# A graph network kernel: twelve node tiles moved to the next gather stage, and a sum moved into a PSUM bank

## The reference

```python
x = _layernorm(x + layer(x, src, dst, ...), axis=-1)
```

## Time and profile before

| what | value |
|---|---|
| median of 3 runs | 2564.44 us (2561.69 to 2572.5) |
| the profiled execution's own time | 2570.28 us |
| its span, first to last instruction | 2568.5 us |
| DVE busy | 1866.1 us (73%) |
| POOL busy | 1429.4 us (56%) |
| PE busy | 1363.8 us (53%) |
| ACT busy | 795.8 us (31%) |
| mean granted PE clock | 0.761 |

### The profile page before, as it was taken

One profiled execution on the slowest core, in us unless ns is written; L12 is line 12 of the kernel. 1 busy time (PEld: TensorE's weight loads), 2 busy tenths in 40 slices (PEclk: granted clock), 3 DMA queues, 4 the chain that ended last, 5 costly groups with the idle time before them and its releaser, 6 DMA issues. The chain is left out here.

```text
span 2568.5 us, 25903 instructions
## 1 busy us (share of the span) xinstructions
PE 1363.8 (53%) x5738; PEld 822.6 (32%) x5738; DVE 1866.1 (73%) x3900; ACT 795.8 (31%) x1636; POOL 1429.4 (56%) x1382
## 2 busy tenths in 40 slices
PE   2443333444766657776467577635888552424241
PEld 1332333332444433332233454411333221212120
DVE  3887777776999957776788699977888675555552
ACT  1232222223666635453122355531232110101010
POOL 6777777745777457773000577720000277777776
PEclk9556666566999979998688799976888665566665
DMA  5433333331333222221011344420000010111110
GB/s 174 121 111 109 110 109 94 107 103 50 93 85 96 75 68 75 75 74 43 22 39 39 88 129 130 126 71 20 28 27 27 29 23 23 24 23 23 23 22 13
DMA packets 120397, 174.74 MB, mean 68 GB/s; under 512 B 36128, under 2 KB 42382, under 8 KB 120340
## 3 DMA queue, kind: packets, MB, share of 16 engines
q1 hardware_dynamic: 74836, 129.98, 15.1%
q0 software_dynamic: 43904, 43.81, 8.7%
q10 hardware_dynamic: 1600, 0.33, 0.1%
HBM read 88.48 MB, written 86.74 MB: 68 GB/s over the span
## 5 line engine op out<-in xcount | busy, mean ns | idle before, releaser
L461 POOL DMA_INDIRECT GA<-table,look_i x588 | 613.1, 1043 | 495.4 <-PEq L1569 213.6
L467 PE MATMUL P<-ident,GA 128*128 128x128 f32 x500 | 104.2, 345 | 404.4 <-DMA GB<-in_x,dst_i 197.3
L491 PE MATMUL P<-center,work 128*128 128x128 f32 x800 | 150.8, 348 | 213.1 <-DVE work L1793 175.7
L266 POOL DMA_INDIRECT GA<-in_x,src_i x196 | 210.2, 1072 | 82.9 <-issue 70.1
L1733 POOL DMA_INDIRECT out_x<-work,seg_i x196 | 205.9, 1051 | 59.8 <-issue 59.8
L1725 POOL DMA_INDIRECT GA<-table,look_i x196 | 201.0, 1026 | 59.8 <-issue 59.4
L266 POOL DMA_INDIRECT GB<-in_x,dst_i x196 | 196.4, 1002 | 59.7 <-issue 59.7
L515 ACT ACTIVATE work<-P 128x512 f32<-128x512 f32 x100 | 59.5, 595 | 512.2 <-PE P L491 512.2
L491 PEld LDWEIGHTS P<-center,work 128*128 128x128 f32 x800 | 133.4, 252 | 244.2 <-issue 115.3
L467 PEld LDWEIGHTS P<-ident,GA 128*128 128x128 f32 x500 | 71.8, 175 | 429.5 <-issue 208.0
L1737 POOL MEMSET GA<- 128x512 f32 x1 | 0.5, 525 | 339.4 <-POOLq L166 339.4
(11 more groups left out here) (349 smaller groups left out, 3498.1 us busy)
## 6 DMA issues: line engine op xcount, KB each, us to landing
table<-work SPq DMA_DIRECT2D x175, 256.0 KB, 2.7
XN<-in_x SPq DMA_DIRECT2D x98, 256.0 KB, 2.8
out_x<-work SPq DMA_DIRECT2D x73, 256.0 KB, 2.1
GA<-table,look_i POOLq DMA_INDIRECT x784, 2.4
XN<-in_src_pad SPq DMA_DIRECT2D x13, 512.0 KB
cols<-in_dst_pad SPq DMA_DIRECT2D x50, 128.5 KB, 4.6
table<-XN SPq DMA_DIRECT2D x1, 6400.0 KB
out_x<-GB SPq DMA_DIRECT2D x25, 256.0 KB, 3.0
```

The lines of the kernel that those rows point to most:

```text
L266: pool.indirect_dma_start(buf[:, s % 2, j * D:(j + 1) * D], None, a["x"], bass.IndirectOffsetOnAxis(ap=look[:, s * 8 + j:s * 8 + j + 1], a ...
L461: pool.indirect_dma_start(GA[:, par, j * D:(j + 1) * D], None, table_k, bass.IndirectOffsetOnAxis(ap=look[:, s * 8 + j:s * 8 + j + 1], axis=0)
L467: ins = pe.transpose(dst[:, q * 128:(q + 1) * 128], src[:, q * 128:(q + 1) * 128], ident[:, :])
L491: ins = pe.matmul(norm_bank(par, far)[:, q * 128:(q + 1) * 128], W[par][4][:, q * 128:(q + 1) * 128], center[:, :], start=True, stop=True)
```

## The change

Node tiles 3, 7, ..., 47 leave the first gather stage, which keeps tiles 1, 5, ..., 49 (13 of them, one for every second edge tile), always in the buffers of parity 0. They are done in the second gather stage, which then has 37 node tiles: its odd slots, empty before, work on every second odd tile (`lent`). In the message stage DVE no longer adds `XD` to the scanned messages; PE centres both, with twice the number of matmuls, and accumulates them in one bank (`norm_pe_sum`). It waits for the second scan in place of the sum. PE's part of that stage is written out in place of the loop. `merge` also takes streams with nothing in them.

```diff
-def paced(eng, S, nodes, owns, unrolled=False):
+def paced(eng, S, nodes, owns, unrolled=False, lent=False):
...
-            if n >= 0 and stage is not None:
+            if n >= 0 and stage is not None and not (lent and n % 4 == 1):
                 at_n, turn = (n, 0) if i is None else (4 * i + n, 2 * i)
+                turn = turn + (n // 2 + 1)
+                if lent and n % 4 == 3:
+                    turn = (0 if i is None else i) + (n // 4 + 1)
                 if not isinstance(at_n, int) or at_n < 2 * NS:
-                    going.append(stage(of(S, n % 2), at_n, n % 2, turn + (n // 2 + 1)))
+                    going.append(stage(of(S, n % 2), at_n, n % 2, turn))
...
+        def norm_pe_sum(pe, T, s, par, k):
+
+            yield 0
+            pe.wait_ge(T("scan1"), k)
+            for q in range(4):
+                part = norm_bank(par, False)[:, q * 128:(q + 1) * 128]
+                pe.matmul(part, W[par][7][:, q * 128:(q + 1) * 128], center[:, :], start=True, stop=False)
+                ins = pe.matmul(part, XD[:, bass.ds(s * HW + q * 128, 128)], center[:, :], start=False, stop=True)
+            ins.then_inc(T("centred"), 1)
...
-                return lambda T, n, par, k: stage(T, n, par, k) if is_node(n, base) and not (even and par) else None
+                return lambda T, n, par, k: stage(T, n, par, k) if is_node(n, base) else None
...
-        NX, NV = ([g[:, par, :] for par in range(2)] for g in (XN, GB))
+        NX, NV = XN[:, 0, :], GB[:, 0, :]
...
+        def beside_even(stage):
+
+            return lambda T, s, par, k: stage(T, s, par, k) if par == 0 else iter(())
...
-                pipelined(dve, S0, gate, sums, together(partial(norm_dve, dve), node_first),
-                          together(partial(back_dve, dve, bank=3), node_second))
+                pipelined(dve, S0, gate, sums, together(partial(norm_dve, dve), beside_even(node_first)),
+                          together(partial(back_dve, dve, bank=3), beside_even(node_second)))
...
                     pe.wait_ge(T("node_x"), 16 * k)
-                    older, turn = tile_before(par, k)
                     if not (isinstance(s, int) and s == 0):
-                        pe.wait_ge(S0(f"node_sq1{older}"), turn)
-                    transpose4(pe, NA, NX[par]).then_inc(T("node_xt"), 1)
+                        pe.wait_ge(T("node_sq1"), k - 1)
+                    transpose4(pe, NA, NX).then_inc(T("node_xt"), 1)
...
-                nodes_tensor(pe, S1, 0, (2, states), (3, src_z), (4, dst_z), (5, logits), unrolled=True, even=True)
+                nodes_tensor(pe, S1, 0, (2, states), (3, src_z), (4, dst_z), (5, logits), unrolled=True, lent=True)
...
-                pipelined(pe, S3, None, message, None, partial(norm_pe, pe), partial(back_pe, pe))
+                pipelined(pe, S3, None, message, None, partial(norm_pe_sum, pe), partial(back_pe, pe), unrolled=True)
...
                     seg_scan(dve, T, k, V, F, at(SAME, s), A.mult, A.add)
-                    dve.tensor_tensor(W[par][4], at(XD, s), F, A.add).then_inc(T("u"), 1)
```

More of the change, by code:

```diff
@@ L39, in merge @@
 def merge(*streams):
-    at = [[next(g), i, g] for i, g in enumerate(streams)]
+    at = [[next(g, None), i, g] for i, g in enumerate(streams)]
+    at = [x for x in at if x[0] is not None]
     while at:
@@ L707, in first_of, with only, nodes_sync @@
             return N - SE if is_last(n, base) else (n + base) * SE
-        def only(base, *stages, even=False):
+        def only(base, *stages):
             def of_node(stage):
-                return lambda T, n, par, k: stage(T, n, par, k) if is_node(n, base) and not (even and par) else None
+                return lambda T, n, par, k: stage(T, n, par, k) if is_node(n, base) else None
             return [stage and of_node(stage) for stage in stages]
-        def nodes_sync(sp, S, base, *owns, even=False):
+        def nodes_sync(sp, S, base, *owns, lent=False):
             def load(T, n, par, k):
@@ L727, in nodes_sync, with nodes_tensor, nodes_scalar, nodes_vector @@
                 sp.sem_inc(S(f"out_stored{par}"), 16)
-            paced(sp, S, only(base, load, None, None, None, None, store, even=even), owns)
+            paced(sp, S, only(base, load, None, None, None, None, store), owns, lent=lent)
             count = min(NODES, NG + 1 - base)
-            for par in range(1 if even else 2):
-                sp.wait_ge(S(f"out_stored{par}"), 16 * ((count + 1 - par) // 2 + 1))
-        def nodes_tensor(pe, S, base, *owns, unrolled=False, even=False):
+            for par in range(2):
+                sp.wait_ge(S(f"out_stored{par}"), 16 * ((NS // 2 if lent and par else (count + 1 - par) // 2) + 1))
+        def nodes_tensor(pe, S, base, *owns, unrolled=False, lent=False):
             for par in range(2):
                 pe.sem_inc(S(f"xn_free{par}"), 1)
[L736 to L742, removed]
+            paced(pe, S, only(base, None, partial(node_pe0, pe), partial(node_pe1, pe)), owns, unrolled, lent)
+        def nodes_scalar(act, S, base, *owns, lent=False):
+            paced(act, S, only(base, None, partial(node_act0, act), partial(node_act1, act), partial(node_act2, act), partial(node_act3, act)), owns, lent=lent)
+        def nodes_vector(dve, S, base, *owns, lent=False):
+            paced(dve, S, only(base, None, None, None, partial(node_dve2, dve), partial(node_dve3, dve)), owns, lent=lent)
         def softmax_rows(block, S, logits, weights, K, slope, own):
@@ L1140, in node_first @@
                     dve.wait_ge(T("node_sq1"), k)
-                    dve.tensor_reduce(sm(par, 3), rows(NX[par]), AX, A.add).then_inc(T("node_ss1"), 1)
+                    dve.tensor_reduce(sm(par, 3), rows(NX), AX, A.add).then_inc(T("node_ss1"), 1)
                     yield 5
@@ L1235, in node_first @@
                     act.wait_ge(T("node_mm"), k)
-                    act.activation(NX[par], NA, ACT.Square).then_inc(T("node_sq1"), 1)
+                    act.activation(NX, NA, ACT.Square).then_inc(T("node_sq1"), 1)
                     yield 4
@@ L1261, in node_store @@
                     sp.wait_ge(T("node_out"), k)
-                    sp.dma_start(rows_of(out, (2 * s + 1) * SE), NV[par]).then_inc(T("node_stored"), 16)
+                    sp.dma_start(rows_of(out, (2 * s + 1) * SE), NV).then_inc(T("node_stored"), 16)
                 storing(sp, S0)
-                for par in range(2):
-                    sp.sem_inc(S0(f"node_stored{par}"), 16)
-                pipelined(sp, S0, node_load, None, lambda T, s, par, k: store_table(sp, T, table[1], s, par, k, 6), node_store)
+                sp.sem_inc(S0("node_stored0"), 16)
+                pipelined(sp, S0, beside_even(node_load), None, lambda T, s, par, k: store_table(sp, T, table[1], s, par, k, 6), beside_even(node_store))
                 all_stored(sp, S0)
                 sp.wait_ge(S0("node_stored0"), 16 * (NS // 2 + 2))
-                sp.wait_ge(S0("node_stored1"), 16 * (NS // 2 + 1))
         S0.done()
@@ L1304, in cube @@
                     return stage
-                pass_back(dve, S1, lambda stage: nodes_vector(dve, S1, 0, (2, stage), (3, cube(0)), (4, cube(1)), even=True))
+                pass_back(dve, S1, lambda stage: nodes_vector(dve, S1, 0, (2, stage), (3, cube(0)), (4, cube(1)), lent=True))
             @block.tensor
@@ L1381, in logits @@
                     act.activation(ROW[par][0:4, :], own_bank(par)[0:4, :], ACT.Copy).then_inc(S1(f"row{par}"), 1)
-                nodes_scalar(act, S1, 0, (2, states), (3, square(0)), (4, square(1)), (5, logits), even=True)
+                nodes_scalar(act, S1, 0, (2, states), (3, square(0)), (4, square(1)), (5, logits), lent=True)
             @block.sync
```

23 lines of the change are left out of this document (11 added, 12 removed).

## The result

| | before | after |
|---|---|---|
| median of 20 runs each | 2566.94 us | 2559.24 us |
| ratio, 95% interval | | 0.9964 [0.9956, 0.9972] |
| the profiled execution | 2570.28 us | 2556.7 us |

What follows compares the result with a forecast made beforehand. DVE was taken to bound the first gather and message stages, POOL the second gather stage. Terms -24 + 10 - 9.5 = -23.5 us, against 2564.4, gave 2541 us, range 2528 to 2558.

Steps and rivals of the forecast that it cites:

- What bounds the kernel now: Stage by stage: DVE bounds the first gather stage, POOL's gathers the second, DVE the message stage.
- Part 1: First gather stage: dropping twelve node tiles passes the pace to POOL at 10.8 us a tile; -24 us.
- Part 2: Second gather stage: twelve added node tiles make PE the bound, 22.5 us a pair against 21.9; +10 us.
- The low end of the term, +1: Second gather stage: everything but the tail of the added tiles fits under POOL's pace; +1 us.
- The rival in which the orders of PE and DVE lock: Second gather stage takes the tiles at nearly their DVE price: +24 instead of +10, 2555 us; chance 0.09.
- the sign to look for: Second gather stage: gathers stretch from 268 to about 276 us, pauses released by PE, PE's gather waits nearly vanish.
- The rule on shared ports: Second gather stage: DVE and GpSimd share ports, so added DVE work would slow gathers; rows showed none, no size given.
- Part 3: Message stage: DVE's dropped sum gives -14, PE's second centring pass costs 2, the end 2.5; -9.5 us.
- The rule on the clock: Extra PE work raises the message stage's clock, returning 2 and 2.5 us; first gather stage drops below 0.93; not counted.
- Sum and base: Whole kernel: -24 + 10 - 9.5 = -23.5 us, against 2564.4, the median of three runs, gives 2541 us.
- the two limits set for the forecast: Forecast is wrong if the first gather stage gains under 15 us or the second loses over 20.
- The slower rival: Message stage: PE becomes the bound at half clock, 8.7 us a tile, +44 instead of -9.5, 2595 us; chance 0.04.

Runs made afterwards that it cites:

- e3: Kernel after with the old message stage and node tiles 3, 7, ..., 47 done in no stage; ratio to kernel before 0.9915, median 2547.41 us.
- e10: Kernel after with ACT doing the lent tile's bias early and copying the scanned states after XS is kept; ratio to kernel before 0.9894, 2540.79 us.
- e8: Kernel before with only PE's message-stage loop written out; one run, 2567.36 us, message stage 187.3 us.
- e4: Kernel after with ACT doing the lent tile's bias ahead of the copy of the scanned states; ratio to kernel before 0.9937, 2551.98 us.
- e9: Kernel after with ACT's copy of the scanned states to XD moved behind the XS copy; ratio to kernel before 0.9926, 2551.47 us.

## Why the prediction was wrong

**What bounds the kernel now** held: DVE in the first gather stage, POOL in the second, DVE in the message stage.

**Part 1, right.** -24 was forecast, -21.8 measured, -21.8 again by time in e3. The gathers lost their nine pauses and run at 264.7/195 x 8 = 10.9 us a tile (10.8 taken); `L1149` waits for PE's transposes, 23.5 us in 15 tiles, as stated. With everything 1.8 us later since the setup, the last `L1149` stands at 872.4 in before's time, for 871.6. DVE is busy 85% for the 90% of the forecast. The miss is in the tail: 20.3 us from there to the next stage, where 21.0 less 2.5 was counted; the halves that are gone saved 0.7.

**Part 2, the step that failed.** The sum said that PE, at 22.5 us a pair, would replace POOL at 21.9, and with 1.5 for the full half-slot on DVE that was 8.5 us before the tail. What was measured is 23.5 us a pair, and 15.6 us up to the last scan (289.5 for 273.9); the tail cost 1.8 for the 1.5 counted. The sum's base, 19.7 us for two own tiles, was not PE's work: PE is busy 161.91 of 220 us there, 16.1 in a pair, and the rest are waits and issue. PE is not full after the change either (80%), and e10 has the same work on it at 21.90 a pair, so a sum of PE's work could not give the number, whatever its terms. The sentence that went wrong besides took 0.6 us *off* "because the dense part is ordered ahead of `L1327`". The dense part waits for ACT's bias (`L659`), and that stands in ACT's queue behind a copy that waits for DVE's scans. For a lent tile this wait is new, and of every added operation it must be asked what its input is queued behind. The low end of the term, +1, was sound as a bound of the work itself: e10 reaches it (+0.2) with the same work in another order on ACT. The rival in which the orders of PE and DVE lock (+24, 2555 us, chance 0.09) named the right mechanism, and on the result it came nearest. It named PE and DVE; ACT's order was in the ring too, and the two edits that opened it are both on ACT. Also wrong was the sign to look for: the gathers were to stretch to 276 us, but two slots hid most of that, and the loss shows behind the last gather.

**The rule on shared ports** (the Trainium skill, SBUF — State Buffer, "Who interferes with whom") was to slow the gathers if it bore on them. The added tiles do not show it: the median gather takes 0.945 us with twelve more node tiles beside it (0.944 before), and in e10, where POOL sets the pace, 196 gathers start within 265.9 us (892.6 to 1158.5), 1.364 us each against 1.373 before. The medians hide the long gathers, though, and those stand beside DVE's scans: of the 156 gathers between 940 and 1160 in the kernel after 50 take over 1.05 us, and 44 of these overlap a scan (48 of 50 before, 940 to 1180). The scans are the same in both kernels, so this changes no term here; SP's transfers start in the same places, and which of the two lengthens a gather was not taken apart. The page itself limits the rule to GpSimd instructions that read SBUF; no run here shows which accesses a gather makes.

**Part 3, right in kind, a little small.** -11.1 for -9.5. The tiles stand (1398.9 - 1246.7)/24 = 6.34 us apart, for 6.3 forecast, which gives -12.2; the bare end costs 1.1 (16.9 us from the last product to DVE's first scan of the next stage, 15.8 before) where 2.5 was counted. The unrolled loop costs nothing (e8).

**The rule on the clock.** The granted clock rose in the message stage from 0.84 to 0.95 and fell in the first gather stage from 0.93 to 0.86, where PE has 3.0 instructions per us (565 in 190) for 3.6 (719 in 200). The Trainium skill (TensorE: Matmul & The Clock Gate, "HAM oscillation") had the direction of both. The message stage gained 1.6 us more than the sum without that rule; of its last two centrings one ran at the half level, where both did before, but no run separates the clock's part. In the first gather stage the lower clock hides under POOL.

**Sum and base.** Of the 18.2 us between 2541 and 2559.24, the profiled executions make 9.9: 2.2 in the first stage, 7.4 in the second, -1.6 in the message stage, and 1.9 elsewhere, where the change touches nothing. Another 5.8 was taken off because before's profiled execution lay so much above a median of three; with 20 runs that is 3.3. And after's profiled execution lies 2.5 *below* its own median. The longer pattern of the message stage, 6 us, would make such a difference if some of the timed runs are in it; the timed runs were not profiled, so that stays open. Neither of the two limits set for the forecast was passed (the first stage gained more than 15, the second lost less than 20 us): they were too wide to catch an error of 7.4 in one term, the largest part of the miss. The slower rival (PE the bound of the message stage, 2595 us) did not come: 7.4 us a tile was its point, 6.34 was measured.

## What to carry to other kernels

A stage in which three engines are each at 80% can be bound all the same, by a ring of waits through queues that each run in order; measure one period in the timeline and walk it backwards, since no sum of busy time shows it. For every operation that a change adds, look up where it stands in its engine's queue and what the instruction ahead of it waits for: here two reorderings on ACT, with no work taken away, were worth more (some 17 us) than the whole change (9 us). And when a place in the pipeline looks empty, try it before believing it: moving pieces to the lighter half-slot lost 25.5 and 39.5 us. And judge an edit like e4 pair by pair, beside the granted clock of each, before its theory is dropped: the gain stood in three pairs and was taken back in eight.

## What the runs showed that was not expected

- The two edits gave more together than their sum: the early bias (e4) brought 3.3 us, the late copy (e9) 12.2, both (e10) 17.2, back to POOL's pace. In e4 the granted clock was 0.93 in eight of eleven pairs, in e9 and e10 1.00 between 940 and 1150.
- A stage behind two gather slots can fall 17 us back while its gathers stretch by only 4.5; the rest is in the tail.
- The same 25 tiles of the message stage took 176.7 us at a granted clock of 0.89 or 182.7 at 0.85. The old form of the stage took 187.1 to 188.2 at 0.80 or 0.81. That PE, brought close to the bound, now makes the stage depend on the clock is likely by this, and not shown.
- Writing out a loop of 25 tiles on PE neither cost nor gave anything (187.3 against 187.8 us).
